# The down products of a gated block, turned around: weights stationary, 512 tokens moving, in high and low parts

## The reference, cut to what matters

```python
xn = _layernorm(x)
s = _L0_attn_ref(xn, ...)                 # 16 heads of 16, 4 key/value heads, softmax over 512 keys, @ Wo
gate, up = split(xn @ w_gate_up.T)        # 256 -> 2 x 1024
h = silu(gate) * up                       # 1024 tokens x 1024
out = h @ w_down.T                        # 1024 -> 256: the down products
g = silu(out)
x = x + s * g
```

## Time and profile before

| what | value |
|---|---|
| time, median of 3 runs | 341.17 us (337.93 to 341.29) |
| the profiled execution: its time, its span | 341.24 us, 339.1 us |
| PE busy | 93% of the span |
| DVE, ACT, POOL busy | 67%, 47%, 20% |
| first attention with its filler | about 30 to 226 us |
| TensorE at half clock | 178.2 to 185.05 us |

### The profile page before, as it was taken

One profiled execution on the slowest core, in us unless ns is written; L12 is line 12 of the kernel. 1 busy time (PEld: TensorE's weight loads), 2 busy tenths in 40 slices (PEclk: granted clock), 3 DMA queues, 4 the chain that ended last, 5 costly groups with the idle time before them and its releaser, 6 DMA issues.

```text
span 339.1 us, 4822 instructions
## 1 busy us (share of the span) xinstructions
PE 316.4 (93%) x1602; PEld 185.9 (55%) x1602; DVE 227.4 (67%) x494; ACT 158.4 (47%) x293; POOL 66.7 (20%) x90
## 2 busy tenths in 40 slices
PE   2989999899999999999999999999999999999990
PEld 2655564455555545455564456546655677765550
DVE  3998867796565667868973773128799666453872
ACT  1484457466767455555364464532406622223230
POOL 5009624600020000000000001300231441117132
PEclk9999999999999999999995999999999999999997
DMA  7900073082280641300000005105954897034621
GB/s 263 402 6 2 0 163 91 2 188 66 63 192 2 135 118 22 106 0 4 1 0 3 0 0 189 63 0 212 366 185 111 288 416 308 15 125 146 242 92 37
DMA packets 19323, 39.19 MB, mean 116 GB/s; under 512 B 1666, under 2 KB 15203, under 8 KB 18016
## 3 DMA queue, kind: packets, MB, share of 16 engines
q1 hardware_dynamic: 17904, 35.69, 33.0%
q0 software_dynamic: 1392, 3.15, 2.6%
HBM read 34.02 MB, written 15.22 MB: 145 GB/s over the span
## 4 chain that ended last, share of the span: by engine, by line
PE 79%; DVE 11%; issue 3%; DMA 3%; ACT 2%; POOL 0%; DVEq 0%; SPq 0%; POOLq 0%; ACTq 0%
PE ps L1797 10%; PE ps L1739 10%; PE ps L1707 9%; PE ps L1810 8%; PE ps L1729 8%; PE ps L1852 5%; PE ps L1868 4%; PE ps L1880 4%; PE ps L1607 3%; PE ps L1548 3%; DVE nmax L1275 3%; PE ps L1640 3%; PE ps L1917 2%; PE ps L1586 2%; DMA cst<-in_const 1%
## 5 line engine op out<-in xcount | busy, mean ns | idle before, releaser
L1275 DVE TENSOR_REDUCE nmax<-ps 128x1 f32<-128x512 f32 x128 | 85.4, 688 | 38.9 <-PE ps L1707 37.9
L1004 ACT ACTIVATE shared<-ps 128x512 f32<-128x512 f32 x128 | 73.8, 594 | 42.2 <-PE ps L1729 41.1
L1707 PE MATMUL ps<-experts 96*128 96x512 bf16 x128 | 48.4, 389 | 2.3 <-DVE experts L1282 1.1
L1729 PE MATMUL ps<-experts 99*128 99x512 bf16 x128 | 49.3, 390 | 0.0
L1810 PE MATMUL ps<-shared,experts 128*128 128x256 f32 x128 | 37.8, 386 | 0.1
L1739 PE MATMUL ps<-shared,experts 128*32 128x512 f32 x256 | 35.0, 619 | 0.3 <-ACT shared L1004 0.3
L1707 PEld LDWEIGHTS ps<-experts 96*128 96x128 bf16 x128 | 12.5, 99 | 37.0 <-DVE nmax L1275 18.4
L1810 PEld LDWEIGHTS ps<-shared,experts 128*128 128x128 f32 x128 | 23.2, 191 | 8.5 <-issue 2.5
L1012 ACT ACTIVATE experts<-ps 96x1024 bf16<-96x1024 bf16 x18 | 18.2, 1020 | 11.4 <-PE ps L1640 11.3
L1607 PE MATMUL ps<-late_weights,xnT 128*128 128x512 f32 (+1 forms) x64 | 22.5, 492 | 0.4 <-DVE shared L1181 0.4
L1852 PE MATMUL ps<-experts,shared 128*128 x88 | 21.0, 382 | 1.6 <-ACT shared L1079 1.6
(11 more groups left out here) (234 smaller groups left out, 534.1 us busy)
## 6 DMA issues: line engine op xcount, KB each, us to landing
experts<-in_experts SPq DMA_DIRECT2D x8, 1536.0 KB, 13.3
slot_rows<-in_empty SPq DMA_DIRECT2D x4, 2080.0 KB, 11.5
shared<-in_wgu SPq DMA_DIRECT2D x1, 2048.0 KB, 10.8
x<-in_x SPq DMA_DIRECT2D x2, 512.0 KB, 5.4
shared<-in_wdn SPq DMA_DIRECT2D x1, 1024.0 KB, 12.8
expert_results<-in_empty SPq DMA_DIRECT2D x1, 1024.0 KB, 6.9
token_rows<-x SPq DMA_DIRECT2D x1, 1024.0 KB, 16.3
token_rows<-gx SPq DMA_DIRECT2D x1, 1024.0 KB, 4.5
```

The lines of the kernel that those rows point to most:

```text
L1004: nc.scalar.activation(probs[:, n % 2, hh, :], ps[:, 2 + hh % 2, :], ACT.Exp, scale=float(HD) ** -0.5).then_inc(s["exp_done"], 1)
L1275: nc.vector.tensor_reduce(nmax[:, 4 * t + hh:4 * t + hh + 1], ps[:, m % 2, :], AX, ALU.max, negate=True).then_inc(s["max_done"], 1)
L1707: nc.tensor.matmul(ps[:, m % 2, :], qs[0:KS, b, GR * g + hh, P * t:P * t + P], ks[0:KS, b, g, :], start=True, stop=True).then_inc(s["score ...
L1729: nc.tensor.matmul(ps[:, 2 + hh % 2, :], ks[0:KM, b, g, P * t:P * t + P], qs[0:KM, b, GR * g + hh, :], start=True, stop=True).then_inc(s[" ...
```

## The change: what it does

The down products of a batch now give 256 output features (two halves `c` of 128) by 512 tokens. An item `("down", 2b+c, i)` holds three fp32r matmuls with a 128x128 part of the down weights stationary and 512 tokens of `hT` moving. There are 32 items where there were 64. The weights are cut in two halves (`round_down`: ACT L1060, POOL L878). Every tile of `hT` is cut into a high and a low part (`h_parts`: ACT L1070, POOL L884), with `PARTS = 4` places for high parts, taken from `x_high` and `x_low`. After the last item of a half, ACT and DVE work on 128x512 instead of 128x256. Then `("back", ...)`, four per kernel of four fp32 transposes each (L1909), turns the tiles back, and an ACT copy (L1075) writes `gx`. The two backs of the second batch stand at the head of `end`. POOL's walk through the plan now decides where it does `h_parts`, the second batch's `x_low` and the router's centring. POOL's preparation of the second batch's queries and keys waits before its last part for the second `max_parts`, and three DVE copies (`slots`) move a few places later.

```diff
+        if kind == "back":
+            return [("product", item[1] // 2 * 2 + 1)]
         if kind in ("gate", "up", "down"):
             bank = {"gate": "bank6", "up": "bank7"}.get(kind, "bank" + str(6 + item[1] % 2))
-            return [(bank,)] if item[2] == 0 else []
+            parts = [("h_low", NI * (item[1] // 2) + item[2])] if kind == "down" else []
+            return parts + [(bank,)] if item[2] == 0 else parts
...
-        for j in range(TB):
-            fill += [("down", b * TB + j, i) for i in range(NI)]
-    cost = {"gate": 3, "up": 3, "down": 2}
+        fill += [("down", 2 * b + c, i) for i in range(NI) for c in range(2)]
+        fill += [("back", 2 * b + c, 0) for c in range(2)]
+    late_back = fill[-2:]
+    del fill[-2:]
+    cost = {"gate": 3, "up": 3, "down": 3, "back": 3}
...
+        if f[0] == "down":
+            while coming and coming[0][1] <= NI * (f[1] // 2) + f[2]:
+                part()
         plan.append(f)
         if f[0] == "up":
             plan.append(("gated", f[1]) if f[2] == 0 else ("hidden", f[1]))
-        return plan[-1]
+            if f[2] and f[1] % NI == NI - 1:
+                coming.extend(("h_parts", f[1] - NI + 1 + i) for i in range(PARTS))
+        if f[0] == "down" and f[1] % 2 and f[2] < NI - PARTS:
+            coming.append(("h_parts", NI * (f[1] // 2) + f[2] + PARTS))
...
         clock.run(item)
         plan.append(item)
+        if coming and item[0] == "prob" and (item[1] % TB, item[2]) not in ((2, 1), (2, 2), (2, 3), (3, 0)):
+            part()
...
             for stage in range(4):
+                if stage == 3:
+                    pool.wait_ge(s["mparts_ready"], 2)
                 prepare(1, None, stage, pool, nc.gpsimd, chain)
...
+            def lower_h(c):
+
+                pool.wait_ge(s["h_high_ready"], c + 1)
+                b, i = divmod(c, NI)
+                nc.gpsimd.tensor_tensor(h_low(i), hT[:, i, :], h_high(b, i).bitcast(F32), ALU.subtract).then_inc(s["h_low_ready"], 1)
...
+                elif kind == "h_parts":
+                    b, i = divmod(it[1], NI)
+                    if i < PARTS:
+                        act.wait_ge(s["up_ready"], NI * (b + 1))
+                    else:
+                        act.wait_ge(s["down_ready"], 2 * (NI * b + i - PARTS + 1))
+                    bk, n = bank_use[("up", it[1])]
+                    act.wait_ge(free_sem[bk], n + 1)
+                    nc.scalar.activation(h_high(b, i), hT[:, i, :], ACT.Copy).then_inc(s["h_high_ready"], 1)
...
-                    ins = nc.tensor.matmul(ps[:, bk, 0:D], hT[:, i, P * (j % TB):P * (j % TB) + P], wdn[:, i, :],
-                                           start=i == 0, stop=i == NI - 1)
+                    if c == 0:
+                        pe.wait_ge(s["h_low_ready"], NI * b + i + 1)
+                    w_parts = [w[:, P * c:P * c + P] for w in (down_high(i), down_low(i))]
+                    h_parts = [h_high(b, i), h_low(i)]
+                    for n_, (w_, h_) in enumerate(((0, 0), (0, 1), (1, 0))):
+                        ins = nc.tensor.matmul(ps[:, bk, :], w_parts[w_], h_parts[h_], start=i == 0 and n_ == 0, stop=i == NI - 1 and n_ == 2)
```

More of the change, by code:

```diff
@@ L124 @@
 FIRST_STACKS = 5
+PARTS = 4
 SLACK, AHEAD = 2, 16
 class Clock:
-    PE = {"prob": .22, "score": .22, "values": .9, "stack_T": .45, "gate": .65, "up": .65, "down": .43, "heads_norm": .43, "max_rows": .22,
+    PE = {"prob": .22, "score": .22, "values": .9, "stack_T": .45, "gate": .65, "up": .65, "down": .69, "back": .6, "heads_norm": .43, "max_rows": .22,
           "attn_T": .43, "wo": 1.7, "wo_half": 1.7, "rows_T": .43, "logits": 3.4, "counts": .4}
@@ L136, in __init__ @@
     def __init__(self):
-        self.now = {"pe": 0., "act": 0., "dve": 0.}
+        self.now = {"pe": 0., "act": 0., "dve": 0., "pool": 0.}
         self.done = {}
@@ L182, in run @@
         elif kind == "down" and item[2] == NI - 1:
-            self.other("act", .27, ("tanh",), t)
-            self.other("dve", .34, ("bank" + str(6 + item[1] % 2),), self.done[("tanh",)])
+            self.other("act", .6, ("tanh",), t)
+            self.other("dve", .69, ("product", item[1]), self.done[("tanh",)])
+        elif kind == "back":
+            self.other("act", .6, ("bank" + str(6 + item[1] % 2),), t)
+        elif kind == "h_parts":
+            self.other("act", .6, ("h_high", item[1]))
+            self.other("pool", 1.25, ("h_low", item[1]), self.done[("h_high", item[1])])
+        elif kind == "round_down":
+            self.other("act", 1.1, ("rounded",))
         elif kind == "heads_out":
@@ L271, in attention_plan, with part @@
     plan = []
+    clock = Clock()
+    coming = []
+    def part():
+        clock.run(coming[0])
+        plan.append(coming.pop(0))
     def emit():
@@ L331, in attention_plan @@
         for hh in range(GR):
-            pace = start + (total - start) * (GR * n + hh + 1) / (GR * STEPS)
+            pace = start + (total - start) * (GR * n + hh + 1) / (GR * STEPS - 3)
             items = [("prob", n, hh)]
@@ L515, in x_low, with down_high, down_low, h_high @@
             return x_low_words[:, TOK * k + S * b:TOK * k + S * b + S]
+        def down_high(i):
+            half = down_high1 if i >= NI // 2 else down_high0
+            return half[:, D * (i % (NI // 2)):D * (i % (NI // 2)) + D]
+        def down_low(i):
+            return w_low_words[:, 2 * KD * INTER + D * i:2 * KD * INTER + D * i + D]
+        def h_high(b, i):
+            a = i % PARTS
+            return x_high(b, a) if a < KD else x_low(b, a - KD)
+        def h_low(i):
+            return h_low_words[:, S * i:S * i + S]
         weight_pieces = [(k, INTER * half) for half in range(2) for k in range(KD)]
@@ L569, in two_gated_blocks @@
                 b_ = (2 if it[1] == 2 else 6) + int(it[0] == "up")
-            elif it[0] == "down" and it[2] == 0:
+            elif it[0] in ("down", "back") and it[2] == 0:
                 b_ = 6 + it[1] % 2
@@ L648, in prepare @@
             if stage == 0:
[L649 removed]
+                eng.wait_ge(s["projections_copied"], 6 if b else group + 1)
                 if turn:
@@ L834, in scatter @@
                         in_=xn[:, j, :], in_offset=None).then_inc(s["scattered"], 16)
-            scatter(0)
+            for it in plan:
+                kind = it[0]
+                if kind == "round_down":
+                    lower_down(it[1])
+                elif kind == "round" and it[2] == KD - 1:
+                    lower_rows(1)
+                elif kind == "h_parts":
+                    lower_h(it[1])
+                elif kind == "logits":
+                    pool.wait_ge(s["router_mean"], 1)
+                    mean = small[:, 1, 0:E].rearrange("p (o e) -> p o e", o=1)
+                    nc.gpsimd.tensor_tensor(router_c[:], router[:], mean.to_broadcast([P, KD, E]), ALU.subtract).then_inc(s["router_centred"], 1)
+                elif kind == "place":
+                    scatter(0)
             scatter(1)
@@ L1362, in _ @@
                     dve.wait_ge(s["wo_ready"], n + 1)
-                    for a in (0, 1):
-                        bk, k_ = bank_use[("down", j + a)]
-                        dve.wait_ge(free_sem[bk], k_ + 1)
+                    bk, k_ = bank_use[("back", 2 * b + c)]
+                    dve.wait_ge(free_sem[bk], k_ + 1)
                     t = gx[:, j:j + 2, :].rearrange("p j n -> p (j n)")
```

111 lines of the change are left out of this document (65 added, 46 removed).

## The result

The changed kernel takes **350.98 us** (median of 4 runs, 349.43 to 351.68) against 340.53 us (4 runs, 337.93 to 341.29) for the kernel before: ratio 1.033 with a 95% interval of 1.029 to 1.037, slower. The forecast was 349.2 in a range of 343 to 352.5. The profiled execution took 351.54 us with a span of 349.7, where before had 341.24 and 339.1: 10.6 us of span to account for.

What follows compares the result with a forecast made beforehand. It took PE (TensorE), busy 93% of the span, to bound the kernel. Terms -3.3 - 1.3 + 3.1 + 3.0 + 2.2 + 0.4 + 0.5 = +4.6 on 341.24 gave 345.8; +3.4 for the clock gave 349.2 us, range 343 to 352.5.

Steps and rivals of the forecast that it cites:

- PE's own work: On PE, down products removed (-27.5), fp32r triples (+22.4) and backs (+1.8) added: -3.3 us.
- POOL kept away from `max_parts`: Second unit's `max_parts` near 61 us: POOL waits, DVE's parts get shorter, PE's standstill goes: -1.3 us.
- The three waits: PE waits for low parts of h, twice in the first batch, once in the second: +3.1, +3.0, +2.2 us.
- ACT's load: Added ACT work mostly under PE, tight only between `values 5` and `values 7`: +0.4 us.
- The end: Last two `values` 2.5 us apart instead of 3.25, losing part of the saving already counted: +0.5 us.
- the backs are in the sum already: Backs run behind `values 31`; their 1.8 us are already counted in PE's work, nothing further added.
- The clock: One fall to half clock at the first two standstills, expected to add 3.4 us.
- standstills, but no further fall: Rival: PE stands still at the waits but the clock does not fall again: 345.8 us, chance 0.25.
- A long slow stretch: Rival: half clock holds from first standstill past the second and returns in the second batch: 352.6 us, chance 0.13.
- The standstills do not cost: Rival: ACT or DVE backlog passes beneath PE's waits, leaving only the savings: 337.1 us, chance 0.12.

Runs made afterwards that it cites:

- e6: Changed kernel with two high parts per batch placed early, a planner holding down products until low parts are there, and the second batch's backs before the last `values`: 335.59 us.
- e4: Kernel before, with only POOL waiting for the second `max_parts` before its last four instructions on the second batch's queries and keys: 338.45 us, ratio 0.996.
- e3: Changed kernel with the second batch's two backs ahead of the last `values` instead of behind it: 349.74 us, ratio to before 1.030.
- e2: Changed kernel with the first two high parts of each batch placed directly behind the last up item: 338.82 us, ratio to before 0.998.
- e1: Changed kernel with 13, 11 and 9 matmuls of no use placed in PE's three waits for low parts: 345.28 us, ratio to before 1.014.
- e5: Changed kernel with useless matmuls in the second and third wait only, the first left idle: 347.43 us, ratio to before 1.025.

## Why the prediction was right, step by step

The direction and the mechanism came out as forecast, and so did the time, 349.2 against 350.98, though with terms missed on both sides of it. The terms in turn:

- **PE's own work, -3.3: a little less, -2.8.** The timeline of the changed kernel shows a down item behind a `stack_T`:

```profile
110.96 0.48 PE L1898 MATMUL ps<-xn,experts 128*128 128x512 f32 x1
111.28 0.39 PE L1898 MATMUL ps<-experts 128*128 128x512 f32 x1
111.50 0.40 PE L1898 MATMUL ps<-xn,shared 128*128 128x512 f32 x1
111.74 0.39 PE L1815 MATMUL ps<-experts 99*128 99x512 bf16 x1
```

  111.74 - 110.96 = 0.78 us for three. Behind a `score` or `prob` an item starts 0.03 us after it and takes 0.89, which is 0.70 once that neighbour has its own 0.22. So what a triple takes depends on what stands before it. Free of this is the sum over everything that PE starts between the first and the last `values`, each from its start to the next, less the waits and the half of the time at half clock: 166.2 us before, 162.3 in the changed kernel with the first batch's two backs, and 163.4 in e6, which has all four. 163.4 - 166.2 = -2.8, and 2.0 us of backs (foreseen 1.8) are in it.
- **POOL kept away from `max_parts`, -1.3: right.** The wait of 1.33 us is gone; from `values 1` to `values 2` it is 5.16 us instead of 6.57, and e4 gives -1.5 alone. The Trainium skill, in "SBUF — State Buffer", section "Who interferes with whom", says that casts of DVE in a two-port mode and its operations with two inputs in SBUF contend with GpSimd for a pair of ports, and that the one which comes later is blocked for a whole instruction. The traces agree. In the earlier trace rows POOL's subtraction ends at 63.09 and the cast begun beside it at 63.13, after 1.24 us; in e6 the two end at 83.95 and 83.99, after 1.12 us of cast; apart from POOL it is 0.17.
- **The three waits, 3.1 + 3.0 + 2.2: right in place and mechanism.** 3.06, 2.53 and 2.15, sum 7.7 for 8.3. I had booked the second too long by half a microsecond, with ACT still behind on exponents; in the timeline above ACT is idle when the `max_rows` transposes end, and the wait is 2.54 also in e3, where PE ran at full clock up to there. e2, which only moves parts in the list, takes two of them away and most of the third: they came from the order, not from load.
- **ACT's load, +0.4: nothing.** Before the last `values` PE has no wait for ACT in the attention of the changed kernel; in e2, where PE runs without the long waits, there is one of 0.36 us.
- **The end, +0.5: right, +0.7**: the last `values` wait 0.96 us for an exponent, before it was 0.25, and the two are 2.56 us apart where I had 2.5. But "the backs are in the sum already" left out that the next user of their banks waits for the copies out of them: **+0.8**, missed. e3 gives it back.
- **Small waits, not in the sum: +0.6.** A `score` waits for DVE's maximum, and a `stack_T` 0.17 us for nothing that the profile shows; neither wait is in the trace before.

```profile
123.39 0.39 PE L1793 MATMUL ps<-experts 96*128 96x512 bf16 x1 [0.41 <-DVE nmax L1366]
```

- **The clock, +3.4: mis-sized.** I counted one fall. In the profiled execution each of the three standstills brought one, 4.8 us net of the stretch at the router, which was 3.4 us shorter than before; by e1's 5.7 us for the three it is 4.0 net. The first fall alone cost 1.6 us in e5, where it was half as long.

These make -2.8 - 1.3 + 7.7 + 0.7 + 0.8 + 0.6 + 4.8 = +10.5 of the 10.6 us of span. The 0.1 left is the time ahead of the first `values`. The same terms fit e6, whose span is 6.2 us shorter than before (332.9 against 339.1): -2.8 of work, -1.3 at `max_parts`, -0.25 for the last exponent (the backs fill that wait), +0.6 of small waits, +0.3 for the exponent at 82.42 and -3.4 for the fall of before make -6.9 up to the last `values`, as measured. The rest is ahead of the first `values` (+0.2) and behind the last (+0.5).

So the forecast put 8.0 us on top of before, and the profiled execution has 10.6. Short were the clock by 1.4, the projection by 0.8, the small waits by 0.6, PE's own work by 0.5 and the end by 0.2; too long were the waits at L1898 by 0.6 and ACT by 0.4. Some of these cancel, so it is in part luck that the median lies only 1.8 us above the forecast. Of the rivals, "standstills, but no further fall" (345.8) is what e1 made by hand, 345.28; in the changed kernel the falls came. "A long slow stretch" fits in time (352.6) but not in form: the clock came back at 90.88, ahead of the second standstill, and what was added were separate falls. "The standstills do not cost" (337.1) fell, since PE found no part ready; e6 with its 335.59 shows that it came near what the change is worth once the parts and the backs stand early.

On the gate of the clock, this case's traces show falls in or behind standstills of 3.06 us (changed kernel, e5), 2.54 (e3), 2.53 and 2.15 (changed kernel), and in one execution, e3, none behind its first of 3.06 and its third of 2.15. The Trainium skill's "TensorE: Matmul & The Clock Gate", section "HAM oscillation", has only longer idle gaps do harm; by that rule the changed kernel would have come to 345.8. The measurement decides: shorter ones cost here too, some 5.5 us for three.

## What to carry to other kernels

A list that every engine walks in order must place the producers of an operand some items ahead of the item that uses it: emitted together with its user, a chain ACT, POOL, PE costs its whole length (2.2 to 3.1 us here) although ACT and POOL have time to spare, and moving two items per batch in the list was worth 12.2 us. Price a standstill of the engine that bounds the kernel at more than its length: here 7.7 us of waits brought another 5.5 or so through the clock, and this share can be measured by filling the waits with matmuls whose result nobody uses. When new work borrows banks, look for who uses them next, and count the copies that empty them.

## What the runs showed of the hardware that was not expected

- The half-clock stretches in these traces came in two lengths, 3.41 to 3.42 and 6.83 to 6.85 us, and the same place had either (6.83 in the changed kernel, 3.42 in e5, none in e3). The 8-column matmuls brought 6.85 us before, 3.41 in the changed kernel, and none in e6.
- A standstill of 2.15 us was followed by half clock in the changed kernel and not in e3, and one of 3.06 us was in the changed kernel and in e5 and not in e3. The 1.33 us of the earlier trace rows and the 1.19 us of e2 were not followed by it.
- A cast of 128x16 on DVE takes 0.17 us, and 1.12 to 1.24 where POOL is in a two-input subtraction, in two places of two kernels. DVE's maximum from the matmul banks took no longer beside POOL: in e6 all 128 of them took 0.68 to 0.70 us, the two beside POOL's subtraction at 81.44 among them.
